# A selective-scan and expert block on one core: dt written twice by TensorE, loads moved inside the unit, the end of the head in a new order

## The reference

```python
xz = x @ in_proj_w.T
xh, z = jnp.split(xz, 2, axis=-1)
xc = _silu(depthwise_conv3x3(xh) + conv_b)             # (B, DI, H, W)
xs = the four orders of xc's positions                 # (B, K, DI, L)
x_dbl = jnp.einsum('bkdl,kcd->bkcl', xs, x_proj_w)
dts, Bs, Cs = jnp.split(x_dbl, [R, R + N], axis=2)
dts = jnp.einsum('bkrl,kdr->bkdl', dts, dt_projs_w)
dts = jax.nn.softplus(dts + dt_projs_b[None, :, :, None])
As = -jnp.exp(A_logs).reshape(K, DI, N)

def step(h, inp):
    u_t, d_t, B_t, C_t = inp
    dA = jnp.exp(d_t[..., None] * As)
    h = h * dA + (d_t * u_t)[..., None] * B_t[:, :, None, :]
    y = jnp.einsum('bkcn,bkn->bkc', h, C_t)
    return (h, y)

y = sum over the directions, each turned back          # then + Ds * xs
y = (layer_norm(y) * out_norm_g + out_norm_b) * _silu(z)
return y @ out_proj_w.T
```

## Time and profile before

| what | value |
|---|---|
| time, median of 3 runs | 1577.3 us (1574.91 to 1587.61) |
| the profiled execution's own time | 1595.89 us |
| its span, first to last instruction | 1594.1 us |
| mean granted TensorE clock | 0.938 of full |
| first scan step of VectorE | 188.57 us from the span's start |
| last scan step of VectorE | 1306.0 us |
| TensorE, VectorE, ScalarE, GpSimd busy | 85%, 77%, 64%, 64% |
| DMA, mean over the span | 95 GB/s |

### The profile page before, as it was taken

The page is one execution under the profiler, slowest core; times in us unless marked ns, Lnnn a source line. Parts: engine busy times, 40 slices in busy tenths (PEclk is TensorE's granted clock), DMA queues, the critical chain, the costliest instruction groups (busy, mean ns, idle before and its releaser), DMA issues. The chain is left out here.

```text
span 1594.1 us, 66411 instructions
## 1 busy us (share of the span) xinstructions
PE 1351.7 (85%) x30388; PEld 830.5 (52%) x30388; DVE 1229.5 (77%) x1029; ACT 1018.5 (64%) x1957; POOL 1025.6 (64%) x294
## 2 busy tenths in 40 slices
PE   6997688888987888998788899878889886969998
PEld 5734455554554555555555555545555543535554
DVE  4876198989899898989989997997989884644220
ACT  3448677777778778787877877776787551311222
POOL 0002089989899998999899998988899980000000
PEclk8998879999999999999999999998999997789999
DMA  9243524233333423333342332334243326100111
GB/s 324 97 156 145 170 56 112 76 93 82 81 87 89 109 79 93 79 90 81 89 113 78 91 99 70 85 85 109 66 101 80 97 82 221 67 0 35 40 40 45
DMA packets 73479, 151.13 MB, mean 95 GB/s; under 512 B 33238, under 2 KB 41942, under 8 KB 72816
## 3 DMA queue, kind: packets, MB, share of 16 engines
q1 hardware_dynamic: 73200, 146.88, 32.1%
HBM read 101.76 MB, written 32.51 MB: 84 GB/s over the span
## 5 line engine op out<-in xcount | busy, mean ns | idle before, releaser
L1219 POOL TENSOR_TENSOR s_h<-s_h,s_crow 128x2048 f32<-128x2048 f32 (+1 forms) x256 | 880.1, 3468 | 159.3 <-DVE s_h L1183 159.3
L1183 DVE TENSOR_TENSOR_SCAN s_h<-s_a,s_pb 128x1024 f32<-128x1024 f32 x384 | 862.4, 2275 | 131.7 <-PE s_pb L1018 96.3
L1018 PE MATMUL s_pb<-k_area,m_dtut 64*64 64x64 f32 x24576 | 479.2, 226 | 149.6 <-DVE s_h L1183 98.7
L1018 PEld LDWEIGHTS s_pb<-k_area,m_dtut 64*64 64x64 f32 x24576 | 435.4, 139 | 325.1 <-DVE s_h L1183 161.9
L1058 PE MATMUL s_py<-s_h,k_eye 64*64 64x512 f32 x3072 | 431.7, 614 | 14.6 <-issue 8.3
L298 ACT ACTIVATE k_area<-k_mask,m_bt 128x64 f32<-128x64 f32 x992 | 273.3, 337 | 0.0
L1109 ACT ACTIVATE s_a<-y_y,m_aneg 128x1024 f32<-128x1024 f32 x192 | 219.0, 1142 | 54.1 <-DVE s_h L1183 53.9
L1109 ACT ACTIVATE s_a<-m_dup,m_aneg 128x1024 f32<-128x1024 f32 x192 | 219.3, 1143 | 32.5 <-DVE s_h L1183 32.5
L204 POOL TENSOR_TENSOR k_area<-m_bt,k_mask 128x2048 f32<-128x2048 f32 x33 | 145.0, 4396 | 128.9 <-ACT m_bt L273 128.9
L1058 PEld LDWEIGHTS s_py<-s_h,k_eye 64*64 64x64 f32 x3072 | 93.2, 138 | 41.4 <-issue 35.6
L270 ACT COPY y_y<-m_pm 128x384 f32<-128x384 f32 x60 | 28.8, 479 | 79.0 <-PE m_pm L224 79.0
(11 more groups left out here) (190 smaller groups left out, 1234.3 us busy)
## 6 DMA issues: line engine op xcount, KB each, us to landing
s_crow<-scratch_xd SPq DMA_DIRECT2D x256, 256.0 KB, 4.1
k_area<-in_x_dram SPq DMA_DIRECT2D x4, 1536.0 KB, 7.9
scratch_xt<-y_y SPq DMA_DIRECT2D x4, 1536.0 KB, 8.6
y_y<-y_y SPq DMA_DIRECT2D x24, 256.0 KB, 4.3
m_dup<-m_dup SPq DMA_DIRECT2D x24, 256.0 KB, 4.2
out_dram<-t_out SPq DMA_DIRECT2D x32, 192.0 KB, 1.9
k_area<-scratch_xt SPq DMA_DIRECT2D x3, 1536.0 KB, 6.8
scratch_xd<-h_dbl SPq DMA_DIRECT2D x8, 512.0 KB, 2.6
```

The source lines that it names most:

```text
L1018: mm = pe.matmul(pb[par * HALF:(par + 1) * HALF, step % 2, r * BANK + blk:(r + 1) * BANK:BLK], dtut[here, u % 2, blk, g * HALF:(g + 1) * H ...
L1183: nc.vector.tensor_tensor_scan(h[:, step % (TRIPLES * CG), f], a[:, step % RING, f], pb[:, step % 2, f], 0.0, ALU.mult, ALU.add).then_inc( ...
L1219: nc.gpsimd.tensor_tensor(here, here, c.unsqueeze(1).broadcast_to([P, groups.stop - groups.start, L]), ALU.mult).then_inc(hc_ready, 1)
```

## The change

dt is no longer doubled by DMA. There are six DUP chunks in steps 15 to 20, one for each group g and half of the positions r. In each, for 8 blocks, TensorE turns the same 64 channels twice: by a matmul with the identity into partitions 64 to 127 and by a transpose into partitions 0 to 63. ScalarE copies all 128 partitions at once. The decay of a group waits for that group's second chunk instead of for a DMA. `double` and its semaphores go.

In the scan, SyncE loads rows two units ahead after the C rows of n = 4 (unit 1's still at the beginning of unit 0), the turned u after n = 4 of a unit with o = 0 and s = 0, and the next image's u after n = 5 of a unit with o = 1 and s = 0.

In the head, TensorE and ScalarE do pair 0's x projections earlier, z tiles and dt projections in turns, and end with pair 1's x projections (with the last z tile between their two halves) and then the six DUP chunks. The table set with both exp and ln is loaded once, ahead of the first exponent. VectorE does softplus and dt before the last convolution. GpSimd begins its mask products when dt x u is done. SyncE's stores are reordered to match.

```diff
@@ chunks_of, chunk_slot @@
-    return order + [("DUP", i) for i in range(4)]
+    return order + [("DUP", i) for i in range(2 * CG)]
-    ... "UT": (5, 7, 10, 13), "DUP": (16, 17, 18, 19)}[what][i]
+    ... "UT": (5, 7, 10, 13), "DUP": (15, 16, 17, 18, 19, 20)}[what][i]
@@ Units.double is removed @@
@@ Units.chunk @@
         if what == "DUP":
             pe.wait_ge(self.dt_ready, ROUNDS * (u + 1))
-            r, chans = i % 2, slice(0, P) if i < 2 else slice(P, DI)
+            g, r = i // 2, i % 2
             here = slice(r * HALF, (r + 1) * HALF)
             for blk in range(BLK):
-                mm = pe.transpose(pm[0:chans.stop - chans.start, blk::BLK], self.dt_of[here, blk, chans], eye[here, here])
+                group = self.dt_of[here, blk, g * HALF:(g + 1) * HALF]
+                pe.matmul(pm[HALF:P, blk::BLK], group, eye[here, here], start=True, stop=True)
+                mm = pe.transpose(pm[0:HALF, blk::BLK], group, eye[here, here])
@@ Units.take_chunk @@
         if what == "DUP":
-            cols = halves()[i % 2]
-            if i < 2:
-                nc.scalar.copy(self.dup[u % 2][HALF:P, 1, cols], pm[HALF:P])
-            dst, src = self.dup[u % 2][0:HALF, 0 if i < 2 else 2, cols], pm[0:HALF]
+            dst, src = self.dup[u % 2][:, i // 2, halves()[i % 2]], pm[:]
@@ head, TensorE @@
             in_proj_x(1, (2,))
+            x_proj(0, (1, 2))
             pe.wait_ge(shared["kept_in"], 16 * len(KEPT))
             m.chunk(pe, 0, "Z", 0)
+            in_proj_z(1, range(0, 1))
+            m.chunk(pe, 0, "Z", 1)
             in_proj_x(1, (0,))
...
             for i in range(4):
                 m.chunk(pe, 0, "UT", i)
-                in_proj_z(1, range(i, i + 1))
+                in_proj_z(1, range(i + 2, i + 3))
+            in_proj_z(1, range(6, 7))
             x_proj(1, (0, 1))
-            in_proj_z(1, range(4, 5))
-            m.chunk(pe, 0, "DUP", 0)
+            in_proj_z(1, range(7, TT))
             x_proj(1, (2, 3))
-            m.chunk(pe, 0, "DUP", 1)
-            in_proj_z(1, range(5, 6))
-            m.chunk(pe, 0, "DUP", 2)
-            in_proj_z(1, range(6, 7))
-            m.chunk(pe, 0, "DUP", 3)
-            in_proj_z(1, range(7, TT))
+            for i in range(2 * CG):
+                m.chunk(pe, 0, "DUP", i)
@@ head, ScalarE @@
-            for part in range(3):
-                m.exponent(act, 0, part)
-            act.wait_ge(m.exp_ready, 1)
+            act.preload_act_table_set("natural_log_exp_and_others")
+            m.exponent(act, 0, 0)
+            m.exponent(act, 0, 1)
+            take_xd(0, 3)
+            m.exponent(act, 0, 2)
...
+            for at in range(2):
+                take_xd(1, at)
             silu_z(1, range(7, TT))
+            for at in range(2, PROJ):
+                take_xd(1, at)
+            for i in range(2 * CG):
+                m.take_chunk(act, 0, "DUP", i)
@@ head, VectorE @@
-            for kind in KINDS:
-                convolve(dve, 1, kind)
+            convolve(dve, 1, 2)
+            convolve(dve, 1, 0)
...
+            convolve(dve, 1, 1)
             m.times_u(dve, 0)
@@ head, GpSimd @@
+            pool.wait_ge(m.dtu_ready, 1)
             for piece in range(2):
                 m.build_d(pool, nc.gpsimd.tensor_tensor, 0, piece)
@@ scan, SyncE @@
-                    if n == 0 and u + 1 < UNITS:
-                        sp.wait_ge(chunk_done, CHUNK[u, "BT", 0] + 1)
-                        load_rows(sp, d, keep, shared, u + 1)
-                        if s == 1 and o == 0:
-                            sp.wait_ge(chunk_done, CHUNK[u - 1, "UT", 3] + 1)
-                            load_u(sp, d, keep, shared, b, "turned")
-                        if s == 1 and o == 1:
-                            sp.wait_ge(y_taken, 2 * (taken(b, 0) + 1))
-                            load_u(sp, d, keep, shared, b + 1, "flat")
+                    for soon in [1] if u == 0 and n == 0 else [u + 2] if n == 4 and u + 2 < UNITS else []:
+                        sp.wait_ge(chunk_done, CHUNK[soon - 1, "BT", 0] + 1)
+                        load_rows(sp, d, keep, shared, soon)
+                    if n == 4 and s == 0 and o == 0:
+                        sp.wait_ge(chunk_done, CHUNK[u, "UT", 3] + 1)
+                        load_u(sp, d, keep, shared, b, "turned")
+                    if n == 5 and s == 0 and o == 1 and b + 1 < BATCH:
+                        sp.wait_ge(y_taken, 2 * (taken(b, 0) + 1))
+                        load_u(sp, d, keep, shared, b + 1, "flat")
...
-                    if n == 6 and u + 1 < UNITS:
-                        m.double(sp, u + 1, range(2))
-                    if n == 7 and u + 1 < UNITS:
-                        m.double(sp, u + 1, range(2, CG))
@@ scan, ScalarE, decay @@
-                    act.wait_ge(dup_in[g], 16 * (u + 1))
+                    act.wait_ge(chunk_taken, CHUNK[u, "DUP", 2 * g + 1] + 1)
```

More of the change, by code:

```diff
@@ L95, in chunk_slot @@
 def chunk_slot(what, i):
-    return {"Z": (0, 1, 2, 3), "BT": (4,), "UT": (5, 7, 10, 13), "DUP": (16, 17, 18, 19)}[what][i]
+    return {"Z": (0, 1, 2, 3), "BT": (4,), "UT": (5, 7, 10, 13), "DUP": (15, 16, 17, 18, 19, 20)}[what][i]
 def u_load(b, what):
@@ L195, in __init__ @@
         self.b_row = sem("b_row")
-        self.dup_in = [sem(f"dup_in{g}") for g in range(CG)]
     def build_d(self, eng, tt, u, piece):
@@ L206, in build_d @@
            self.keep["mask"][:].unsqueeze(1).broadcast_to(shape), ALU.mult).then_inc(self.d_odd if piece % 2 else self.d_even, 1)
[L208 to L214, removed]
     def chunk(self, pe, u, what, i):
@@ L483, in head @@
         order = [("T", b, c) for b in range(3) for c in range(NC)] + [("X", 0, kind) for kind in KINDS]
-        order += [("T", 3, c) for c in range(NC)] + [("P", 0, 0)] + [("X", 1, kind) for kind in KINDS]
-        order += [("P", 0, at) for at in range(1, PROJ)] + [("P", 1, at) for at in range(PROJ)]
+        order += [("T", 3, c) for c in range(NC)] + [("P", 0, 0), ("X", 1, 2), ("P", 0, 1), ("P", 0, 2), ("X", 1, 0), ("P", 0, 3), ("X", 1, 1)]
+        order += [("P", 1, at) for at in range(PROJ)]
         def big_of(*use):
@@ L545, in _ @@
             store_u(1, 0)
+            store_z(1, 0, TT // 2)
             store_u(1, 1)
[L547 to L552, removed]
+            for at in range(2):
+                store_xd(1, at)
             store_z(1, TT // 2, TT)
+            for at in range(2, PROJ):
+                store_xd(1, at)
             for b in range(BATCH):
@@ L763, in _ @@
             fill_xpad(1, 2)
+            take_xd(0, 1)
             for b in range(2, BATCH):
@@ L767, in _ @@
             m.take_chunk(act, 0, "Z", 0)
+            take_xd(0, 2)
+            silu_z(1, range(0, 1))
+            m.take_chunk(act, 0, "Z", 1)
             fill_xpad(1, 0)
-            m.take_chunk(act, 0, "Z", 1)
-            fill_xpad(1, 1)
             m.take_chunk(act, 0, "Z", 2)
-            take_xd(0, 1)
+            silu_z(1, range(1, 2))
             m.take_chunk(act, 0, "Z", 3)
-            for part in range(3):
-                m.exponent(act, 0, part)
-            act.wait_ge(m.exp_ready, 1)
+            act.preload_act_table_set("natural_log_exp_and_others")
[3 more added lines that the diff above has]
+            m.exponent(act, 0, 2)
             nc.scalar.activation(m.lnz, m.ez, ACT.Ln, bias=1.0).then_inc(m.ln_ready, ROUNDS)
@@ L781, in _ @@
             nc.scalar.mul(m.aneg[:], m.amin[:], -1.0).then_inc(m.aneg_ready, 1)
-            take_xd(0, 2)
+            fill_xpad(1, 1)
             m.take_chunk(act, 0, "BT", 0)
-            take_xd(0, 3)
+            silu_conv(1, 2)
             for i in range(4):
                 m.take_chunk(act, 0, "UT", i)
-                silu_z(1, range(i, i + 1))
-                if i < 2:
-                    silu_conv(1, KINDS[i])
+                silu_z(1, range(i + 2, i + 3))
+                if i == 1:
+                    silu_conv(1, 0)
+            silu_z(1, range(6, 7))
             silu_conv(1, 1)
-            take_xd(1, 0)
-            take_xd(1, 1)
-            silu_z(1, range(4, 5))
-            m.take_chunk(act, 0, "DUP", 0)
-            take_xd(1, 2)
-            take_xd(1, 3)
-            m.take_chunk(act, 0, "DUP", 1)
-            silu_z(1, range(5, 6))
-            m.take_chunk(act, 0, "DUP", 2)
-            silu_z(1, range(6, 7))
-            m.take_chunk(act, 0, "DUP", 3)
+            for at in range(2):
+                take_xd(1, at)
             silu_z(1, range(7, TT))
+            for at in range(2, PROJ):
+                take_xd(1, at)
+            for i in range(2 * CG):
+                m.take_chunk(act, 0, "DUP", i)
             act.wait_ge(turned, NC * BATCH)
```

12 lines of the change are left out of this document (5 added, 7 removed).

## The result

The changed kernel takes 1975.3 us in the median (1973.75 to 1979.84, 4 runs) where the kernel before, beside it, took 1582.5 (4 runs): ratio 1.247, 95% interval 1.242 to 1.252. It is slower by a quarter. The profiled execution took 1973.75 us with a span of 1972.0, 377.9 us more than the span before.

What follows compares the result with a forecast made beforehand. VectorE sets the scan's pace, with TensorE only some 0.3 us a step to spare. Scan 311 + head 15 - relief 25 = +301 us, added to the 1577.3 median: 1878 us, range 1750 to 2150.

Steps and rivals of the forecast that it cites:

- The mechanism: In TensorE's dt chunks, alternating matmul and transpose costs time at each change; later B products queue behind and VectorE waits.
- the clock: TensorE's granted clock falls to half in each unit's first two chunks and the step between, then returns to full.
- the head: Before the scan: x projections taken until 172.7 us, then six chunk copies, two rounds at half clock; ends 14.6 us later.
- the relief: At unit ends, moved loads and dropped doubling DMAs cut VectorE's waits for TensorE: 25 us taken, between 0 and 53.
- steps 16 to 21 of 15 units: Scan steps delayed by the six new chunks: 20.7 us a unit, 311 us in all.
- The chunk at full clock: TensorE's time for one new dt chunk in the scan: 3.2 us, taken between 2.9 and 3.6.
- The two differences of the earlier trace: TensorE's rows before the change: 0.11 us to enter a transpose chunk from plain matmuls, 0.07 us to leave.
- rival D: Both column tiles run side by side on TensorE, a chunk takes 0.98 us, no change: 1572 us; chance 0.18.
- the first part: First two chunks of a unit and the step between at half clock: 5.3 + 3.62 + 5.3 = 14.2 us.
- the second: Four further rounds of a unit at full clock, each 1.84 us plain step plus 3.2 us chunk: 20.2 us.
- The signs: Profile would show 24-record chunks of 2.9 to 3.6 us, longer VectorE waits, lower clock, units near 89, first scan near 203.

Runs made afterwards that it cites:

- The runs with 2, 8 and 16 changes: Order of a dt chunk's matmuls and transposes in the changed kernel: eight then eight 1664.4 us, two then two 1744.1 us, alternating (unedited) 1975.3 us.
- the grouped version: Changed kernel with all 8 matmuls of a dt chunk issued first, then all 8 transposes: 1664.4 us, ratio 1.052.
- the split versions: Changed kernel with each scan chunk halved around the y sums: 2111.4 us; also one step later: 1839.6 and 2096.6; or step 15's B product issued four times: 2002.3.
- the later version: Changed kernel with each scan chunk halved around the y sums and chunks behind steps 16 to 21 instead of 15 to 20: two executions, 1839.6 and 2096.6 us.

## Why the prediction was right, and where its sizes were off

It said slower, 1878 us, range 1750 to 2150; it came to 1975. The mechanism is the one that it named, and three terms were mis-sized: the clock by 75 us and the head by 8 too little, and against them the relief by 15 too little. That these partly cancel is luck.

| term, us on the profiled execution | predicted | measured |
|---|---|---|
| steps 16 to 21 of 15 units | 311 | 386 |
| head | 14.6 | 22.9 |
| relief, all waits for B but those of steps 16 to 21 | -25 | -40 |
| elsewhere | 0 | 9 |
| sum | 301 | 378 |

Of the 40 us of relief, 9.3 are waits that steps 19 to 21 had before, which now stand within the 386. The 9 us elsewhere are 6 in the scan, where VectorE's scans take 2.29 us each when they stand alone and were 2.18 apart back to back, and 2.5 in the tail. The sums differ by 77 us and the forecast by 97: the other 20 aren't of the change, since the profiled execution of before was 18.6 us over the 1577.3 to which the forecast was added, and that of after 1.6 under its median.

**The chunk at full clock** was right: taken as 3.2 between 2.9 and 3.6, measured 3.43. The two differences of the earlier trace rows, 0.11 to enter and 0.07 to leave, stood for 0.13 each. The Trainium skill, TensorEngine Tiling (Array Packing), Key Properties and Restrictions, has a change of tiling mode drain the engine and denies fp32 transposes the column tiling. The runs with 2, 8 and 16 changes (1.59, 2.35 and 3.43 us) agree; what the engine does in a change no trace shows. The Trainium skill, TensorE: Matmul & The Clock Gate, Part 3, has tiles in different column groups run at once. That holds here for two plain matmuls (0.89 us a chunk) and not for a matmul beside a transpose, and rival D goes with it.

**The clock** is the term that failed. The prediction had the first two chunks, with the step between them, at half clock and four rounds at full, 14.2 + 20.2 us. In unit 3 the first part came true: 13.7 us, 546.13 to 559.78. In the second it put 1.84 for each plain step. The chunks did run at full clock, but the products behind each took 3.35 (566.52 to 569.87), and a round 6.78 instead of 5.04: four of these and a last B product at half clock are some 8 us a unit. Five units are like this one, with 27.1 to 27.9 us of waits in steps 16 to 21. In the ten others the second chunk runs at full clock already (VectorE waits 4.4 to 4.5 us before step 17 instead of 6.27), and the waits are 23.9 to 25.4 us. So the first part was too much in two units of three, the second too little in all, and the mean is 25.8 instead of 20.7. The step took the clock for one that, once back, stays; it doesn't where sparse and dense stretches of this length take turns.

**The head** was off by 8.3 us: all five rounds were at half clock, 29.3 us instead of 23.2, and the x projections were taken until 174.9 instead of 172.7, since TensorE wasn't ready with them sooner. **Relief** was larger than taken, and inside its bounds (0 to 53). At the units' ends VectorE's waits fell from 48.2 us to 14.7. The loads' part of this is shown, some 22 us. The other 12 go with the missing doubling and the new chunks; in the grouped version, where VectorE waits far less in steps 16 to 21, 17.2 us are left, so that most of it isn't hidden behind those waits. The doubling alone was not tried.

**The signs** that it named came: 24 records in 3.4 us, waits of 2.5 us or more before each of steps 17 to 21 (4.4 to 6.3), 346 us more for TensorE instead of some 300, the clock below full in each unit's last third (0.70 to 0.76 from step 16 to 21). Two had other sizes: units are (1617.7 - 211.5) / 15 = 93.7 us instead of the 89 named, and the first scan is at 211.5 instead of 203.

## What to carry to other kernels

Before pairing a plain matmul with a transpose in one loop, count the changes between the two kinds: with the 64-wide fp32 tiles of this kernel 16 changes cost 2.1 us and the 24 passes 1.5, and putting like with like, or writing both as plain matmuls, gave back 311 and 349 of 393 us. Where an engine has only 0.3 us a step to spare, a transfer that is off its path can be cheaper than 0.9 us on it: here the version with plain matmuls stayed 41 us behind the doubling. Of a change with several parts, time the small ones alone: here the moved loads were a gain of about 1% that the rest buried.

## What the runs showed of the hardware that was not expected

- Dense products ran at half clock right behind sparse chunks that ran at full (0.51 and 0.99, in turn, for 20 us and more). With chunks of 1.59 or 2.35 us between the same products the clock stayed at 1.00 from step 16 to 21, with the shorter in all 15 units and with the longer, within 0.02, in 13. So here the work that pays for the low clock is the work behind the one that brought it about.
- The same steps can keep either clock: in the split versions the stretch from step 16 to 21 had 1.00 or 0.50 from end to end, in 23 to 26 or in 39 to 43 us. TensorE had been idle for longer just before the stretches at half in general, but not always: of the eight units of the later version with the same idle time before their first half chunk only one fell. What decides there stays open.
